# Attention over rows of 128 tokens: one maximum and one shift for the first group, merged copies of g and of P x, three exponentials ahead of a copy

## The chip, the core and the metric

The kernel runs on one NeuronCore of a Trainium2 chip. The metric is the device time of one execution in microseconds (us). Before the change it is 4721.29 us, the median of three runs (4721.06 to 4724.11). All tensors are 32-bit floats.

The engines that matter: TensorE (PE in the profile; PEld are its weight loads), VectorE (DVE), ScalarE (ACT), GpSimd (POOL), and the queue of SyncE (SP) that issues the DMAs. Each runs its own list of instructions in order, and they wait for one another by semaphores.

## The reference, cut to what matters

```python
xn = (x - moving_mean) * rsqrt(moving_var + 0.001) * gamma + beta   # x: (64, 128, 128, 64)
q = xn @ Wq + bq;  k = xn @ Wk + bk;  v = xn @ Wv + bv
scores = einsum('bhid,bhjd->bhij', q, k) * 64 ** -0.5               # 128 x 128 for each (b, h)
attn = softmax(scores, axis=-1)
out = einsum('bhij,bhjd->bhid', attn, v) @ Wo + bo
return xn + out
```

There are 64*128 = 8192 independent attentions, each over 128 tokens of 64 channels.

## The kernel before

The weights are folded once at the start: with g = (Wq Wk^T)^T x + a bias, the scores of one attention are one product of g and x, and the output is (P x) times one folded matrix, with P the softmax. So the loop never forms q, k or v.

Work comes in groups of 8 attentions (N = 1024 groups), and every engine's list is made of the same steps, one for two groups: the even group 2t and the odd group 2t+1. 512 steps do the work, and each engine's step handles several groups at different stages. `pipeline` (L177) writes out the first 12 steps and the last 8, and loops over bodies of 4 steps between.

What each engine does in a step, in its order:

- TensorE: transposes P of the even group before (`transpose_probs`, into `tg_ps`); scores of the even group (into `score_ps[0]`) and of the odd group (into `score_ps[1]`), the last pair of the odd ones behind a wait; transposes P of the odd group before; P x of two older groups (`probs_times_x`, into `uo_ps[0]` and `uo_ps[1]`, which also gives `u_made`); the two projections g of the next groups (`project`, into the two halves of `tg_ps`); the two output products (`output`, back into `uo_ps`), of which the last pair stands behind a wait for the copies of g, since the transposes that follow overwrite `tg_ps`.
- ScalarE: half of a copy of the transposed P (L349); two exponentials of the even group (L335; an exponential handles one attention, and its bias is `neg_top`, the negated shift of each row); a whole copy of the odd P (L351); the other six exponentials of the even group; two copies of g (`keep_g`, L360); eight exponentials of the odd group. A group's scores may be overwritten only when its eight exponentials are over (`probs_found`).
- VectorE: scaling of an older output by the inverted sums; its half of the copy of the transposed P (L549); inverted sums; then for the even group the maximum of attentions 0 to 3 (L490), their shift (L501), the maximum of attentions 4 to 7 (L490), their shift (L501); the maximum of the odd group in one (L480); the two copies of P x to SBUF (`keep_u`, L521); the shift of the odd group (L511); a transposition of incoming x for two groups (L559); a row constant (L530); and a scaling. In every second step (`vector_adds`) this last scaling is in place (L455) and is followed by the addition of x (L466), which GpSimd does otherwise.
- GpSimd weighs x, adds the bias, and adds x to three outputs in four. SyncE's queue loads x twice in two layouts and stores the results.

`tg_ps` is used in turn by the projections and by both transposes; `uo_ps[0]` and `uo_ps[1]` by P x and by the output product of the same group. `uT` has one place for an even group and one for an odd.

Of the kernel before, what the change touches and what calls it, by code (L numbers as in the profile page):

```python
# [17 lines left out]
def build(nc: bass.Bass, x, gamma, beta, mean, var, wq, bq, wk, bk, wv, bv, wo, bo, out):  # L18
# [12 lines left out]
    with ExitStack() as ctx:  # L31
# [3 lines left out]
        def psum(name, shape=(128, 512)):  # L35
            return ctx.enter_context(nc.psum_tensor(name, list(shape), F32))
# [57 lines left out]
        tg_ps = psum("tg_ps", (128, 2, 512))  # L94
        uo_ps = [psum(f"uo_ps{i}") for i in range(2)]
        score_ps = [psum(f"score_ps{i}", (128, 2, 512)) for i in range(2)]
# [12 lines left out]
        max_found = sem_ring("max_found")  # L109
        max_a_found = sem_ring("max_a_found")  # L110
        max_b_found = sem_ring("max_b_found")
        neg_const_found = sem_ring("neg_const_found")
        neg_top_found = sem_ring("neg_top_found")
        neg_top_a_found = sem_ring("neg_top_a_found")
        neg_top_b_found = sem_ring("neg_top_b_found")
        const_found = sem_ring("const_found")
# [196 lines left out]
        def _(act):  # L313
# [9 lines left out]
            def exponentials(r, n, peeled, rows):  # L323
                if not exists(r, n, peeled):
                    return
                s = parts(n)
                if 0 in rows:
                    act.wait_ge((neg_top_a_found if n % 2 == 0 else neg_top_found)[s], uses(r, n))
                    if exists(r, n - 4, peeled):
                        act.wait_ge(probsT_made[s], uses(r, n - 4))  # L330
                        act.wait_ge(sum_inverted[parts(n | 1)], uses(r, (n - 4) | 1))
                for q in rows:
                    if q == HALF and n % 2 == 0:
                        act.wait_ge(neg_top_b_found[s], uses(r, n))
                    last = nc.scalar.activation(probs[:, n % 4, q, :], score_ps[n % 2][:, q // PAIRS, q % PAIRS * W:(q % PAIRS + 1) * W],  # L335
                                                ACT.Exp, bias=neg_top[:, s, q:q + 1], accum_out=prob_sum[:, s, q:q + 1])
                    if q == GROUP - 1:
                        last.then_inc(probs_found[s], 1)
# [13 lines left out]

            def keep_g(r, n, peeled):
                if not exists(r, n, peeled):
                    return
                s = parts(n)
                act.wait_ge(g_made[s], uses(r, n))
                if exists(r, n - 4, peeled):
                    act.wait_ge(scores_made[s], uses(r, n - 4))
                nc.scalar.activation(g[:, s].rearrange("p k w -> p (k w)"), tg_ps[:, n % 2],  # L360
                                     ACT.Identity, bias=g_bias[:, 0:1]).then_inc(g_kept[s], 1)

            def step(r, t, peeled):
                keep_probsT(r, 2 * t - 2, peeled)
                exponentials(r, 2 * t, peeled, range(0, 2))
                keep_probsT(r, 2 * t - 1, peeled)
                exponentials(r, 2 * t, peeled, range(2, 8))
                keep_g(r, 2 * t + 2, peeled)
                keep_g(r, 2 * t + 3, peeled)
                exponentials(r, 2 * t + 1, peeled, range(0, 8))  # L370

# [3 lines left out]
        def _(dve):  # L375
# [107 lines left out]

            def find_max_half(r, n, peeled, h):
                if not exists(r, n, peeled):
                    return
                s = parts(n)
                if h == 0:
                    dve.wait_ge(scores_made[s], uses(r, n))
                nc.vector.tensor_reduce(row_stat[:, s, h * HALF:(h + 1) * HALF, NEG_MAX],  # L490
                                        score_ps[n % 2][:, h, :].rearrange("p (k w) -> p k w", k=PAIRS),
                                        AX_X, ALU.max, negate=True).then_inc((max_a_found if h == 0 else max_b_found)[s], 1)

            def find_shift_half(r, n, peeled, h):
                if not exists(r, n, peeled):
                    return
                s = parts(n)
                dve.wait_ge((max_a_found if h == 0 else max_b_found)[s], uses(r, n))
                if h == 0:
                    dve.wait_ge(neg_const_found[parts(n | 1)], uses(r, n | 1))  # L500
                nc.vector.tensor_reduce(neg_top[:, s, h * HALF:(h + 1) * HALF],  # L501
                                        row_stat[:, s, h * HALF:(h + 1) * HALF, NEG_MAX:ROW_CONST + 1], AX_X,
                                        ALU.add).then_inc((neg_top_a_found if h == 0 else neg_top_b_found)[s], 1)

            def find_shift(r, n, peeled):
# [7 lines left out]

            def keep_u(r, n, peeled):
                if not exists(r, n, peeled):
                    return
                s = parts(n)
                dve.wait_ge(u_made[s], uses(r, n))
                if exists(r, n - 2, peeled):
                    dve.wait_ge(o_made[parts(n - 2)], uses(r, n - 2))  # L520
                nc.vector.tensor_copy(uT[:, n % 2], uo_ps[n % 2][:].rearrange("p (k w) -> p k w", k=PAIRS)) \  # L521
                    .then_inc(u_kept[s], 1)
# [39 lines left out]
            def step(r, t, peeled):  # L562
# [3 lines left out]
                negate_const(r, 2 * t + 1, peeled)  # L566
                for h in range(2):
                    find_max_half(r, 2 * t, peeled, h)
                    find_shift_half(r, 2 * t, peeled, h)
                find_max(r, 2 * t + 1, peeled)  # L570
                keep_u(r, 2 * t - 4, peeled)
                keep_u(r, 2 * t - 3, peeled)
# [12 lines left out]
        def _(pe):  # L585
# [27 lines left out]
            def scores(r, n, peeled, pairs):  # L613
# [3 lines left out]
                if 0 in pairs:  # L617
                    pe.wait_ge(g_kept[s], uses(r, n))
                    if exists(r, n - 2, peeled):
                        pe.wait_ge(probs_found[parts(n - 2)], uses(r, n - 2))  # L620
# [26 lines left out]
            def await_transposes(r, n, peeled):  # L647
# [7 lines left out]
                if n % 2 == 0:  # L655
                    if exists(r, n + 3, peeled):
                        pe.wait_ge(g_kept[parts(n + 2)], uses(r, n + 2))
                        pe.wait_ge(g_kept[parts(n + 3)], uses(r, n + 3))
                else:
                    pe.wait_ge(probsT_b_kept[parts(n - 1)], uses(r, n - 1))  # L660
# [12 lines left out]
            def project(r, n, peeled):  # L673
# [6 lines left out]
                elif exists(r, n - 2, peeled):  # L680
                    pe.wait_ge(g_kept[parts(n - 2)], uses(r, n - 2))
                nc.tensor.matmul(tg_ps[:, n % 2], w_g_all, xT[:, n % 8].rearrange("p k w -> p (k w)"),  # L682
                                 start=True, stop=True).then_inc(g_made[s], 1)

            def output(r, n, peeled, pairs):
# [3 lines left out]
                if 0 in pairs:  # L689
                    pe.wait_ge(u_kept[s], uses(r, n))  # L690
                for k in pairs:
# [41 lines left out]
```

## Time and profile before

| | us |
|---|---|
| median of 3 runs | 4721.29 |
| the profiled execution's own time | 4727.12 |
| its span in the trace | 4724.9 |
| busy: PE | 4540.1 |
| busy: DVE | 4495.3 |
| busy: POOL | 4508.7 |
| busy: ACT | 4297.6 |

The span is what the trace covers; the execution's own time has some 2 us more around it. Four engines are busy for over 90% of the span, so the table alone names no bound. TensorE was granted its full clock (mean 0.998). A busy figure counts instructions from start to end, and on VectorE and ScalarE the end of one overlaps the start of the next, so the distance from start to start is what an instruction occupies.

### The profile page before, as it was taken

What the parts mean: (1) busy time and instruction counts of PE and PEld (TensorE: products, weight loads), DVE (VectorE), ACT (ScalarE), POOL (GpSimd) and SP (SyncE); (2) the same over time, 40 slices, a digit from 0 to 9 for tenths busy, and PEclk for the clock granted to TensorE, in tenths of its full rate; (3) what the DMA queues carried; (4) which work ended last, traced back from release to release, by engine and by line L of the source; (5) the groups of instructions that cost most, each with busy time, mean ns of one, the idle gap of its engine ahead of it and who ended that gap; (6) DMA issues with size and microseconds to landing.
All of it is one profiled execution on the core that took longest, in us unless ns stands there. A gap on an engine that the chain in (4) does not pass through costs nothing.

```text
span 4724.9 us, 187136 instructions
## 1 busy us (share of the span) xinstructions
PE 4540.1 (96%) x59416; PEld 3778.9 (80%) x59416; DVE 4495.3 (95%) x7970; ACT 4297.6 (91%) x18437; POOL 4508.7 (95%) x2824
## 2 busy tenths in 40 slices
PE   7999999999999999999999999999999999999999
PEld 5888888888888888888888888888888888888887
DVE  7999999999999999999999999999999999999998
ACT  7999999999999999999999999999999999999998
POOL 7999999999999999999999999999999999999998
PEclk9999999999999999999999999999999999999999
DMA  7888888888888888888888888888888888888886
GB/s 141 174 173 172 173 172 172 172 173 172 173 171 172 172 172 172 172 173 173 171 173 173 172 173 171 172 172 172 172 172 172 173 171 172 173 172 173 171 173 139
DMA packets 4294236, 806.28 MB, mean 171 GB/s; under 512 B 4294208, under 2 KB 4294208, under 8 KB 4294208
## 3 DMA queue, kind: packets, MB, share of 16 engines
q1 hardware_dynamic: 4293312, 805.80, 85.3%
q8 instruction: 15, 0.25, 0.0%
q10 hardware_dynamic: 896, 0.13, 0.0%
q14 instruction: 13, 0.11, 0.0%
HBM read 537.10 MB, written 268.44 MB: 170 GB/s over the span
## 4 chain that ended last, share of the span: by engine, by line
ACT 36%; DVE 26%; PE 20%; issue 15%; DVEq 2%; POOL 1%; DMA 0%; ACTq 0%; POOLq 0%
ACT probs L335 29%; PE uo_ps L643 10%; DVE xT L559 7%; PE score_ps L624 6%; ACT probsT L351 5%; DVE row_stat L530 5%; DVE uo_ps L455 4%; DVE probsT L549 3%; DVE row_stat L490 3%; ACT g L360 3%; PE tg_ps L670 3%; DVE attn L446 2%; DVE neg_top L501 1%; DVE inv_sum L473 1%; PE tg_ps L682 1%
## 5 line engine op out<-in xcount | busy, mean ns | idle before, releaser
L335 ACT ACTIVATE probs<-score_ps,neg_top 128x128 f32<-128x128 f32 x8192 | 2890.5, 384 | 301.9 <-DVE neg_top L501 301.9
L277 POOL TENSOR_TENSOR x_weighted<-x_in,row_weights 128x1024 f32<-128x1024 f32 x1024 | 2402.7, 2371 | 21.8 <-DVE x_weighted L433 21.8
L335 ACT ACTIVATION_READ_ACCUMULATOR probs<-score_ps,neg_top 128x1 f32 x8192 | 1835.5, 224 | 0.0
L624 PE MATMUL score_ps<-xT,g 64*128 64x128 f32 x16384 | 1165.3, 281 | 152.3 <-ACT probs L335 152.3
L624 PEld LDWEIGHTS score_ps<-xT,g 64*128 64x128 f32 x16384 | 1015.1, 188 | 236.9 <-issue 235.4
L288 POOL TENSOR_TENSOR x_scaled_rows<-x_weighted,out_bias 128x512 f32<-128x512 f32 x1024 | 1199.9, 1199 | 0.0
L692 PEld LDWEIGHTS uo_ps<-w_o,uT 128*128 128x128 f32 x8192 | 994.9, 192 | 244.0 <-issue 243.7
L299 POOL TENSOR_TENSOR y<-attn,x_scaled_rows 128x512 f32<-128x512 f32 x768 | 982.3, 1279 | 190.8 <-DVE attn L446 190.8
L682 PE MATMUL tg_ps<-xT,w_g 128*128 128x512 f32 x2048 | 1019.2, 620 | 4.7 <-DVE xT L559 3.5
L643 PE MATMUL uo_ps<-probsT,x_in 128*64 128x128 f32 x16384 | 1008.5, 276 | 0.0
L692 PE MATMUL uo_ps<-w_o,uT 128*128 128x128 f32 x8192 | 997.4, 275 | 0.0
L643 PEld LDWEIGHTS uo_ps<-probsT,x_in 128*64 128x64 f32 x16384 | 884.9, 137 | 34.7 <-issue 0.2
L521 DVE COPY uT<-uo_ps 128x512 f32<-128x512 f32 x1024 | 687.8, 687 | 91.4 <-PE uo_ps L643 74.3
L360 ACT ACTIVATE g<-tg_ps,g_bias 128x512 f32<-128x512 f32 x1024 | 706.6, 711 | 45.8 <-PE tg_ps L682 16.9
L670 PE MATMUL tg_ps<-ident,probs 64*128 64x64 f32 x16384 | 719.3, 226 | 5.3 <-ACT g L360 3.2
L490 DVE TENSOR_REDUCE row_stat<-score_ps 128x4 f32<-128x512 f32 x1024 | 699.3, 683 | 17.5 <-PE score_ps L624 0.9
L670 PEld LDWEIGHTS tg_ps<-ident,probs 64*128 64x128 f32 x16384 | 634.4, 139 | 69.2 <-issue 5.6
L559 DVE STREAM_TRANSPOSE xT<-x_quads 128x1024 f32<-128x1024 f32 x512 | 631.5, 1234 | 0.0
L480 DVE TENSOR_REDUCE row_stat<-score_ps 128x8 f32<-128x1024 f32 x512 | 622.6, 1216 | 1.7 <-PE score_ps L624 1.7
L682 PEld LDWEIGHTS tg_ps<-xT,w_g 128*128 128x128 f32 x2048 | 347.8, 189 | 338.3 <-issue 337.7
L530 DVE TENSOR_REDUCE row_stat<-x_weighted 128x16 f32<-128x1040 f32 x512 | 611.2, 1194 | 2.1 <-POOL x_weighted L277 2.1
L351 ACT ACTIVATE probsT<-tg_ps 128x1024 f32<-128x1024 f32 x512 | 524.1, 1024 | 57.3 <-PE tg_ps L670 57.3
(70 smaller groups left out, 2019.1 us busy)
## 6 DMA issues: line engine op xcount, KB each, us to landing
x_quads<-in_x SPq DMA_DIRECT2D x4096, 64.0 KB, 2.2
x_in<-in_x SPq DMA_DIRECT2D x1024, 256.0 KB, 3.2
out<-y SPq DMA_DIRECT2D x1024, 256.0 KB, 2.4
norm_row<-in_L_conv_gamma ACTq DMA_DIRECT2D x1, 32.0 KB, 2.1
norm_row<-in_L_conv_beta ACTq DMA_DIRECT2D x1, 32.0 KB, 3.7
norm_row<-in_L_conv_bo SPq DMA_DIRECT2D x1, 32.0 KB, 3.4
norm_row<-in_L_conv_moving_mean ACTq DMA_DIRECT2D x1, 32.0 KB, 3.3
norm_row<-in_L_conv_moving_var ACTq DMA_DIRECT2D x1, 32.0 KB, 4.6
```

The source lines that it names most:

```text
L277: nc.gpsimd.tensor_tensor(x_weighted[:, n % 4, :, 0:2 * C].rearrange("p s (h c) -> p s h c", h=2), x_in[:, n % 8, :, None, :].broadcast_to ...
L288: nc.gpsimd.tensor_tensor(x_scaled_rows[:, n % 8], x_weighted[:, n % 4, :, 0:C], bias_b, ALU.add).then_inc(x_scaled[s], 1)
L299: nc.gpsimd.tensor_tensor(y[:, s], attn[:, s], x_scaled_rows[:, n % 8], ALU.add).then_inc(y_found[s], 1)
L335: last = nc.scalar.activation(probs[:, n % 4, q, :], score_ps[n % 2][:, q // PAIRS, q % PAIRS * W:(q % PAIRS + 1) * W], ACT.Exp, bias=neg_ ...
L360: nc.scalar.activation(g[:, s].rearrange("p k w -> p (k w)"), tg_ps[:, n % 2], ACT.Identity, bias=g_bias[:, 0:1]).then_inc(g_kept[s], 1)
L530: nc.vector.tensor_reduce(row_stat[:, s - 1:s + 1, :, ROW_CONST], x_weighted[:, s - 1:s + 1, :, C:2 * C + 1], AX_X, ALU.add).then_inc(cons ...
L559: nc.vector.transpose(xT[:, n % 8 - 1:n % 8 + 1].rearrange("p g k w -> p (g k w)"), x_quads[:, n % 8 - 1:n % 8 + 1].rearrange("p g k w -> ...
L624: last = nc.tensor.matmul(score_ps[n % 2][:, h, k * W:(k + 1) * W], g[half, s, k, :], xT[half, n % 8, k, :], start=True, stop=True)
L643: last = nc.tensor.matmul(uo_ps[n % 2][h * C:(h + 1) * C, k * W:(k + 1) * W], x_in[:, n % 8, PAIRS * h + k, :], probsT[:, n % 4, PAIRS * h ...
L670: last = nc.tensor.transpose(tg_ps[:, h, q * C:(q + 1) * C], probs[half, n % 4, q, :], ident[half, half])
L682: nc.tensor.matmul(tg_ps[:, n % 2], w_g_all, xT[:, n % 8].rearrange("p k w -> p (k w)"), start=True, stop=True).then_inc(g_made[s], 1)
L692: last = nc.tensor.matmul(o_pairs[n % 2][:, :, k, :], uT[:, n % 2, k, :], w_o_all, start=True, stop=True)
```

## The change

Four edits, all inside a step:

- VectorE finds the even group's maximum for all eight attentions in one operation of 1024 elements, and its shift in one (`find_max`, `find_shift`), as it does for the odd group. The half versions and their semaphores go. ScalarE's first exponential of the even group waits for that one shift.
- The two copies of P x are one of 128x1024 (`uo_ps` is now one tensor of two banks), which waits for both products. TensorE's two output products wait for that one copy.
- The two copies of g are one of 128x1024, which waits for both projections. It stands behind the first two exponentials of the odd group, where the two copies stood ahead of them.
- Three exponentials of the even group, in place of two, stand ahead of the whole copy of the odd P.

```diff
             def step(r, t, peeled):
                 keep_probsT(r, 2 * t - 2, peeled)
-                exponentials(r, 2 * t, peeled, range(0, 2))
+                exponentials(r, 2 * t, peeled, range(0, 3))
                 keep_probsT(r, 2 * t - 1, peeled)
-                exponentials(r, 2 * t, peeled, range(2, 8))
-                keep_g(r, 2 * t + 2, peeled)
+                exponentials(r, 2 * t, peeled, range(3, 8))
+                exponentials(r, 2 * t + 1, peeled, range(0, 2))
                 keep_g(r, 2 * t + 3, peeled)
-                exponentials(r, 2 * t + 1, peeled, range(0, 8))
+                exponentials(r, 2 * t + 1, peeled, range(2, 8))
...
+                act.wait_ge(g_made[parts(n - 1)], uses(r, n - 1))
                 act.wait_ge(g_made[s], uses(r, n))
...
-                nc.scalar.activation(g[:, s].rearrange("p k w -> p (k w)"), tg_ps[:, n % 2],
+                nc.scalar.activation(g[:, s - 1:s + 1].rearrange("p n k w -> p (n k w)"), tg_ps[:].rearrange("p n x -> p (n x)"),
                                      ACT.Identity, bias=g_bias[:, 0:1]).then_inc(g_kept[s], 1)
...
+                dve.wait_ge(u_made[parts(n - 1)], uses(r, n - 1))
                 dve.wait_ge(u_made[s], uses(r, n))
                 if exists(r, n - 2, peeled):
+                    dve.wait_ge(o_made[parts(n - 3)], uses(r, n - 3))
                     dve.wait_ge(o_made[parts(n - 2)], uses(r, n - 2))
-                nc.vector.tensor_copy(uT[:, n % 2], uo_ps[n % 2][:].rearrange("p (k w) -> p k w", k=PAIRS)) \
+                nc.vector.tensor_copy(uT[:].rearrange("p n k w -> p (n k w)"), uo_both[:].rearrange("p n x -> p (n x)")) \
                     .then_inc(u_kept[s], 1)
...
-                for h in range(2):
-                    find_max_half(r, 2 * t, peeled, h)
-                    find_shift_half(r, 2 * t, peeled, h)
+                find_max(r, 2 * t, peeled)
+                find_shift(r, 2 * t, peeled)
                 find_max(r, 2 * t + 1, peeled)
-                keep_u(r, 2 * t - 4, peeled)
                 keep_u(r, 2 * t - 3, peeled)
...
-                    pe.wait_ge(g_kept[s], uses(r, n))
+                    pe.wait_ge(g_kept[parts(n | 1)], uses(r, n | 1))
...
-                        pe.wait_ge(g_kept[parts(n + 2)], uses(r, n + 2))
                         pe.wait_ge(g_kept[parts(n + 3)], uses(r, n + 3))
...
-                    pe.wait_ge(u_kept[s], uses(r, n))
+                    pe.wait_ge(u_kept[parts(n | 1)], uses(r, n | 1))
```

VectorE in a step with the addition in place, before the change, from the copy of the transposed P to the end of the step (`score_ps0` holds the even group, `score_ps1` the odd; the digit at a semaphore is its place in a ring):

```order
L549 COPY probsT<-tg_ps 128x8x64 [waits u_made0,probsT_made0]
L473 RECIPROCAL inv_sum<-prob_sum 128x16 [waits probs_found3]
L538 TENSOR_REDUCE row_stat<-row_stat 128x16 [waits const_found3]
L490 TENSOR_REDUCE row_stat<-score_ps0 128x4 [waits scores_made2]
L501 TENSOR_REDUCE neg_top<-row_stat 128x4 [waits neg_const_found3,max_a_found2]
L490 TENSOR_REDUCE row_stat<-score_ps0 128x4
L501 TENSOR_REDUCE neg_top<-row_stat 128x4 [waits max_b_found2]
L480 TENSOR_REDUCE row_stat<-score_ps1 128x8 [waits scores_made3]
L521 COPY uT<-uo_ps0 128x512 [waits o_made0,u_made2]
L521 COPY uT<-uo_ps1 128x512 [waits o_made1,u_made3]
L511 TENSOR_REDUCE neg_top<-row_stat 128x8 [waits neg_const_found3,max_found3]
L559 STREAM_TRANSPOSE xT<-x_quads 128x1024 [waits scores_made1,quads_loaded5,quads_loaded4]
```

The same place of VectorE's list after the change:

```order
L529 COPY probsT<-tg_ps 128x8x64 [waits u_made0,probsT_made0]
L471 RECIPROCAL inv_sum<-prob_sum 128x16 [waits probs_found3]
L518 TENSOR_REDUCE row_stat<-row_stat 128x16 [waits const_found3]
L478 TENSOR_REDUCE row_stat<-score_ps0 128x8 [waits scores_made2]
L488 TENSOR_REDUCE neg_top<-row_stat 128x8 [waits neg_const_found3,max_found2]
L478 TENSOR_REDUCE row_stat<-score_ps1 128x8 [waits scores_made3]
L501 COPY uT<-uo_ps 128x1024 [waits o_made0,o_made1,u_made3,u_made2]
L488 TENSOR_REDUCE neg_top<-row_stat 128x8 [waits neg_const_found3,max_found3]
L539 STREAM_TRANSPOSE xT<-x_quads 128x1024 [waits scores_made1,quads_loaded5,quads_loaded4]
```

Four operations on the even group have become two, and the first value of its shift now stands behind a reduction of 1024 elements. The two copies of P x, each with its own `u_made`, have become one that waits for both.

ScalarE over one step before the change, from the first exponential of an even group to the exponentials of the odd one:

```order
L335 ACTIVATE probs,prob_sum<-score_ps0,neg_top 128x128 [waits sum_inverted3,probsT_made2,neg_top_a_found2]
L335 ACTIVATE probs,prob_sum<-score_ps0,neg_top 128x128
L351 ACTIVATE probsT<-tg_ps 128x1024 [waits u_made1,probsT_made1]
L335 ACTIVATE probs,prob_sum<-score_ps0,neg_top 128x128 x2
L335 ACTIVATE probs,prob_sum<-score_ps0,neg_top 128x128 [waits neg_top_b_found2]
L335 ACTIVATE probs,prob_sum<-score_ps0,neg_top 128x128 x3
L360 ACTIVATE g<-tg_ps,g_bias 128x512 [waits scores_made0,g_made0]
L360 ACTIVATE g<-tg_ps,g_bias 128x512 [waits scores_made1,g_made1]
L335 ACTIVATE probs,prob_sum<-score_ps1,neg_top 128x128 [waits sum_inverted3,probsT_made3,neg_top_found3]
L335 ACTIVATE probs,prob_sum<-score_ps1,neg_top 128x128 x7
```

The same stretch of ScalarE after the change:

```order
L330 ACTIVATE probs,prob_sum<-score_ps0,neg_top 128x128 [waits sum_inverted3,probsT_made2,neg_top_found2]
L330 ACTIVATE probs,prob_sum<-score_ps0,neg_top 128x128 x2
L346 ACTIVATE probsT<-tg_ps 128x1024 [waits u_made1,probsT_made1]
L330 ACTIVATE probs,prob_sum<-score_ps0,neg_top 128x128 x5
L330 ACTIVATE probs,prob_sum<-score_ps1,neg_top 128x128 [waits sum_inverted3,probsT_made3,neg_top_found3]
L330 ACTIVATE probs,prob_sum<-score_ps1,neg_top 128x128
L358 ACTIVATE g<-tg_ps,g_bias 128x1024 [waits scores_made0,scores_made1,g_made1,g_made0]
L330 ACTIVATE probs,prob_sum<-score_ps1,neg_top 128x128 x6
```

The copy of g has moved behind two exponentials of the odd group, and these wait for the odd group's shift, which VectorE computes behind the copy of P x.

## Rows read from the trace of the kernel before

**Rows 1.** The head of the profile page: span, and busy time of each engine.

```profile
span 4724.9 us, 187136 instructions
PE 4540.1 (96%) x59416; PEld 3778.9 (80%) x59416; DVE 4495.3 (95%) x7970; ACT 4297.6 (91%) x18437; POOL 4508.7 (95%) x2824
```

**Rows 2.** Chain of waits, from 1996 us on: start us, us on the chain, what.

```profile
1996.24 1.16 PE score_ps L624 x16
...
1999.85 0.04 DVE uT L521
...
2000.46 0.04 DVE neg_top L511
...
2005.79 0.60 DVE row_stat L490
...
2006.61 0.03 ACT probs L335
...
2014.53 1.16 PE score_ps L624 x16
```

**Rows 3.** The same chain near its beginning and near its end, the same piece.

```profile
205.10 1.16 PE score_ps L624 x16
...
4500.21 1.16 PE score_ps L624 x16
```

**Rows 4.** Waits: engine, line waited for: us in total, times, longest us.

```profile
ACT probs L335 <- DVE neg_top L501: 301.9, 510, 1.8
PE score_ps L624 <- ACT probs L335: 152.3, 511, 1.1
DVE uT L521 <- PE uo_ps L643: 74.3, 401, 3.7
```

**Rows 5.** Groups of instructions by line: busy us, mean ns of one, idle before.

```profile
L521 DVE COPY uT<-uo_ps 128x512 f32<-128x512 f32 x1024 | 687.8, 687 | 91.4 <-PE uo_ps L643 74.3
L360 ACT ACTIVATE g<-tg_ps,g_bias 128x512 f32<-128x512 f32 x1024 | 706.6, 711 | 45.8 <-PE tg_ps L682 16.9
...
L490 DVE TENSOR_REDUCE row_stat<-score_ps 128x4 f32<-128x512 f32 x1024 | 699.3, 683 | 17.5 <-PE score_ps L624 0.9
...
L480 DVE TENSOR_REDUCE row_stat<-score_ps 128x8 f32<-128x1024 f32 x512 | 622.6, 1216 | 1.7 <-PE score_ps L624 1.7
...
L351 ACT ACTIVATE probsT<-tg_ps 128x1024 f32<-128x1024 f32 x512 | 524.1, 1024 | 57.3 <-PE tg_ps L670 57.3
...
L349 ACT ACTIVATE probsT<-tg_ps 128x512 f32<-128x512 f32 x512 | 331.5, 648 | 0.0
```

**Rows 6.** Timeline of ScalarE at the copies of g: start us, us, instructions merged.

```profile
2010.27 1.32 ACT L360 ACTIVATE g<-tg_ps,g_bias 128x512 f32<-128x512 f32 x2
2011.47 0.38 ACT L335 ACTIVATE probs<-score_ps,neg_top 128x128 f32<-128x128 f32 x1
...
2011.81 0.38 ACT L335 ACTIVATE probs<-score_ps,neg_top 128x128 f32<-128x128 f32 x1
```

**Rows 7.** Timeline of TensorE and VectorE over the same step and the next start.

```profile
2005.38 1.16 PE L624 MATMUL score_ps<-xT,g 64*128 64x128 f32 x16 [0.29 <-ACT probs L335]
...
2005.70 0.67 DVE L490 TENSOR_REDUCE row_stat<-score_ps 128x4 f32<-128x512 f32 x1
...
2007.29 1.22 DVE L480 TENSOR_REDUCE row_stat<-score_ps 128x8 f32<-128x1024 f32 x1
...
2008.42 1.28 DVE L521 COPY uT<-uo_ps 128x512 f32<-128x512 f32 x2
...
2008.86 1.98 PE L682 MATMUL tg_ps<-xT,w_g 128*128 128x512 f32 x4
...
2009.62 0.17 DVE L511 TENSOR_REDUCE neg_top<-row_stat 128x8 f32<-128x24 f32 x1
...
2013.11 1.11 PE L624 MATMUL score_ps<-xT,g 64*128 64x128 f32 x16
...
2014.27 0.69 DVE L490 TENSOR_REDUCE row_stat<-score_ps 128x4 f32<-128x512 f32 x1
```

More of the change, by code:

```diff
@@ L94, in build @@
         tg_ps = psum("tg_ps", (128, 2, 512))
-        uo_ps = [psum(f"uo_ps{i}") for i in range(2)]
+        uo_both = psum("uo_ps", (128, 2, 512))
+        uo_ps = [uo_both[:, i] for i in range(2)]
         score_ps = [psum(f"score_ps{i}", (128, 2, 512)) for i in range(2)]
@@ L109, in build @@
         max_found = sem_ring("max_found")
-        max_a_found = sem_ring("max_a_found")
-        max_b_found = sem_ring("max_b_found")
         neg_const_found = sem_ring("neg_const_found")
         neg_top_found = sem_ring("neg_top_found")
-        neg_top_a_found = sem_ring("neg_top_a_found")
-        neg_top_b_found = sem_ring("neg_top_b_found")
         const_found = sem_ring("const_found")
@@ L327, in exponentials @@
                 if 0 in rows:
-                    act.wait_ge((neg_top_a_found if n % 2 == 0 else neg_top_found)[s], uses(r, n))
+                    act.wait_ge(neg_top_found[s], uses(r, n))
                     if exists(r, n - 4, peeled):
@@ L332, in exponentials @@
                 for q in rows:
-                    if q == HALF and n % 2 == 0:
-                        act.wait_ge(neg_top_b_found[s], uses(r, n))
                     last = nc.scalar.activation(probs[:, n % 4, q, :], score_ps[n % 2][:, q // PAIRS, q % PAIRS * W:(q % PAIRS + 1) * W],
@@ L356, in keep_g @@
                 s = parts(n)
+                act.wait_ge(g_made[parts(n - 1)], uses(r, n - 1))
                 act.wait_ge(g_made[s], uses(r, n))
                 if exists(r, n - 4, peeled):
+                    act.wait_ge(scores_made[parts(n - 5)], uses(r, n - 5))
                     act.wait_ge(scores_made[s], uses(r, n - 4))
-                nc.scalar.activation(g[:, s].rearrange("p k w -> p (k w)"), tg_ps[:, n % 2],
+                nc.scalar.activation(g[:, s - 1:s + 1].rearrange("p n k w -> p (n k w)"), tg_ps[:].rearrange("p n x -> p (n x)"),
                                      ACT.Identity, bias=g_bias[:, 0:1]).then_inc(g_kept[s], 1)
@@ L482, in find_max @@
                                         AX_X, ALU.max, negate=True).then_inc(max_found[s], 1)
[L484 to L503, printed above, removed]
             def find_shift(r, n, peeled):
@@ L680, in project @@
                 elif exists(r, n - 2, peeled):
-                    pe.wait_ge(g_kept[parts(n - 2)], uses(r, n - 2))
+                    pe.wait_ge(g_kept[parts((n - 2) | 1)], uses(r, (n - 2) | 1))
                 nc.tensor.matmul(tg_ps[:, n % 2], w_g_all, xT[:, n % 8].rearrange("p k w -> p (k w)"),
```

## The prediction, made before the changed kernel ran

> **What bounds the kernel now.** I read the page's head first: four engines between 91% and 96% busy [rows 1]. Shares so close name no bound, and an edit that saves busy time on one engine need not save anything. So the next view is the chain of waits, which shows what really follows what. It repeats every two steps, and its turn is this loop:
>
> - TensorE starts the scores of an odd group at 1996.24; P x of the older odd group is made behind them, and VectorE starts the second copy of P x at 1999.85, 3.61 us later.
> - The copy is over at 2000.46, where the odd shift starts (0.61 us). VectorE then works through its list (transposition, constant, scaling, addition, the next step's scaling and copy) to the first half maximum of the next even group: it starts at 2005.70 [rows 7] (the chain counts it from 2005.79). That is 5.24 us in which VectorE never stands still for another engine.
> - Half a maximum and its shift, and ScalarE starts the first exponential at 2006.61: 0.91 us.
> - ScalarE runs eight exponentials of the even group, a copy, two copies of g, eight of the odd group; when these are over, TensorE may overwrite the odd scores: 2014.53, 7.92 us later, where the loop closes [rows 2].
>
> Sum: 3.61 + 0.61 + 5.24 + 0.91 + 7.92 = 18.29 us for two steps. Over the whole run: from 205.10 to 4500.21 there are 235 such turns, so 18.28 us each [rows 3], and 256 turns are 4679 us of the 4724.9. So this loop is the kernel. It always passes through the same kind of step, the one whose VectorE list has the addition in place. In the other kind VectorE is just in time: the first maximum starts at 2014.27, when the scores started at 2013.11 (1.11 us) are ready [rows 7].
>
> The waits agree with it. ScalarE waits 301.9 us for the shift, 0.59 us a step, and TensorE 152.3 us for the exponentials, 0.30 us a step [rows 4]. Without waiting, TensorE needs from 2005.38 to 2014.22 (2013.11 + 1.11) for all but the last matmuls of a step, 8.84 us [rows 7]. It is close behind but not the bound.
>
> **The change part by part, each on this loop.**
>
> One maximum for the even group. The first exponential now waits for a reduction of 1024 elements, not 512: 1216 ns against 683 ns, by rows of these very shapes [rows 5]. The start comes 0.53 us later: **+0.53 us a turn**. ScalarE is the waiting engine there [rows 4], so nothing hides it. What VectorE gains, the distance from the first half's start to the odd maximum, was 1.59 us (2005.70 to 2007.29) [rows 7] and becomes some 1.22 + 0.17 = 1.39: 0.20 us saved. But that comes ahead of the copy of P x, where VectorE then waits for TensorE. On this loop it is worth nothing.
>
> One copy of P x. The second of two copies (687 ns) started when its product was made; now the whole copy starts then, and the first half, which was done while TensorE made the second product, follows the wait as well. No row shows a copy of 1024 elements on VectorE. The bounds: the 687 ns of the short one (nothing lost), and twice it, 1374 ns. The nearest row is the maximum over the same 1024 elements from the same memory, 1216 ns, whose short form (683) matches the short copy's 687 [rows 5]. I take 1.22 us: 1.22 - 0.69 = **+0.53 us a turn**. Its reward is 0.06 us of VectorE's time where two copies ran back to back (2008.42 to 2009.62 is 1.20 us [rows 7]; one would take about 1.22 less the 0.08 of overlap, 1.14), and again it lies ahead of no late work: behind the copy VectorE's 5.24 us are unchanged, so the next maximum is late by the whole amount. The output products wait for this copy too: it ends 3.61 + 1.26 = 4.87 us behind the start of the odd scores, and TensorE reaches them at 2008.86 + 1.98 - 2005.38 = 5.46. That wait costs nothing, with 0.6 us to spare.
>
> One copy of g. Two copies took from 2010.27 to 2011.47, 1.20 us, and their records end 0.12 us later [rows 6]. The long copy of P on ScalarE takes 1024 ns and the short 648; I add that difference to the 711 ns of a copy of g: 1.09 us, and 0.97 us to the next start [rows 5]. **-0.23 us a turn**. The bounds: 1.20 us (nothing gained) and 0.71 us, the short one's (-0.49).
>
> What a page says of the two merges: the Trainium skill (Perfetto Trace Analysis, Optimizing Scalar/DVE Operations) gives each such instruction a fixed access cost, some 125 ns on VectorE and 51 ns on ScalarE where it reads PSUM, and says that grouping helps "if the engine is saturated". The trace has both engines above 90% busy, and yet ScalarE waits at this point in every step [rows 4], so its condition isn't met where the time is set; by its sum the change would be a gain, which is the faster rival below.
>
> The order on ScalarE. Moving one exponential ahead of the copy of P changes nothing in the sum: the same instructions lie between the first exponential and the last; nothing here waits for the copy soon enough to matter (TensorE needs it only behind both P x products, and 0.35 us later). Moving g behind two exponentials of the odd group likewise keeps the sum, if these find their shift. The shift now comes from the long copy: 3.61 + 0.04 + 1.22 + 0.20 = 5.07 us behind the start of the odd scores. In the loop's step ScalarE reaches them about 6 us behind: the maximum starts there 3.61 + 1.14 + 5.24 = 9.99 us behind the odd scores of the step before, which is 0.9 us behind the next ones if these follow after 9.10; then come 1.44 us to the first exponential, eight exponentials at 0.34 [rows 6] and 0.9 for the copy of P (1.02 less 0.12 of overlap), 5.96 in all. No wait. g then needs both projections, made 5.46 us behind: also there. In the other kind of step the shift is the later one, and ScalarE waits; that loop is priced with the rivals.
>
> **The sum.** 18.28 + 0.53 + 0.53 - 0.23 = 19.11 us a turn, +0.83. With 254 turns (the first and the last two steps are not in the pattern): +211 us. Against the profiled execution, 4727.12 us, that is 4938; the median of the runs shown lies 5.8 us below it, so **4932 us**, 4.5% slower. Its own range comes from the bounds that matter: g between 0.88 and 1.05 to the next start (-23 to +20 us) and the long copy of P x at 1.10 to 1.28 us (-30 to +15): 4880 to 4970. With the far ends of both rows of bounds it would be 4730 (the copy costs nothing more and g gains 0.49) and 5030.
>
> **The rivals.**
>
> Faster: the engines' work carries the time, not this loop. Then VectorE saves 0.20 + 0.06 = 0.26 us a step, ScalarE 0.23, and 512 x 0.26 = 133 us come off: 4588. For it: the busy shares, all over 90% [rows 1], and the copies of P x that start back to back without a wait in one step of two [rows 7], which looks like a VectorE that is late for its work. It decides if the long copy can start on VectorE's own clock in both kinds of step. Against it: DVE waited for P x 401 times in 512 steps [rows 4], and the change makes VectorE arrive earlier and its input complete later. Chance 0.07.
>
> Only one of the two delays counts: the copy of P x gives its time back, say because VectorE's list behind it holds a pause that I can't see. Then 0.53 - 0.23 = 0.30 us a turn, +76: 4797. For it: the chain has pieces named as issue in that stretch. Against: the starts lie as close there as the instructions allow. Chance 0.06.
>
> A new loop is the bound: the odd exponentials ahead of g wait for the shift in every step: 3.61 + 1.26 + 0.20, two exponentials 0.69, g 0.97, and six exponentials with their end (2011.47 to 2014.53 less 0.69) 2.37: 9.10 us for one step, 18.20 for two. Less than 19.11, so it only shapes the other step. It would need 0.46 us more a step to decide; and TensorE's transposes, which wait for g, then follow at 6.9 us behind the maximum. If these close a loop with the late step that I haven't priced, the turn grows by up to the 0.5 us between them, +60 to +130 us: about 5025. Chance 0.03.
>
> No change: the two delays fall into pauses and g's gain is cancelled too: 4721, chance 0.03.
>
> **How the numbers follow.** Forecast 0.81, faster rival 0.07, one delay 0.06, new loop 0.03, no change 0.03. A measurement of this kernel can't tell less than about 0.2% (9 us) from no change. Faster by more: 0.07. Same: 0.03. Slower: 0.81 + 0.06 + 0.03 = 0.90. The range 4860 to 4980 holds the forecast's own with some room and leaves out the other cases, 0.19 together; to take in one more of them it would have to reach 4797.
>
> **What would show it.** ScalarE's wait for the shift grows from 302 us to about 600 to 700, part of it now ahead of the odd exponentials. VectorE's wait for P x grows from 74 us to some 300: in one kind of step it arrives 1.2 us early, in the other hardly. TensorE's wait for the exponentials goes to about 400. The chain shows the same loop with 19.1 us, with pieces of 1.2 us for the copy and the even maximum. Lines: even maximum 1.22 us, copy of P x 1.22, copy of g 1.09. The prediction is wrong if the turn isn't about 19.1 us or the chain leaves the copy of P x; its terms are wrong if the long copy takes much less than 1.2 us.

## The result, and the profile of the changed kernel

The changed kernel takes **4954.69 us** (median of three runs, 4954.67 to 4954.86), against 4721.29: a ratio of 1.0493, 95% interval 1.0469 to 1.0516. It is slower by 233 us. The forecast was 4932. One execution of one of the kernels below (`g_only`) ran at a granted clock of 0.851 and took 5265 us; it is left out of that kernel's figure.

The head of its page, beside [rows 1]:

```profile
span 4952.5 us, 184581 instructions
PE 4671.2 (94%) x59416; PEld 3843.6 (78%) x59416; DVE 4357.8 (88%) x6434; ACT 4147.0 (84%) x17925; POOL 4505.2 (91%) x2824
```

VectorE's busy time fell by 138 us and ScalarE's by 151 us, and the span rose by 228 us. The merges did save engine time; none of it shows.

Waits (engine, line waited for: us in total, times, longest), to be read beside [rows 4]; L330 is the exponential, L488 the shift, L501 the copy of P x, L621 P x, L346 the whole copy of the transposed P, L659 the projection:

```profile
ACT probs L330 <- DVE neg_top L488: 762.9, 512, 3.7
...
DVE uT L501 <- PE uo_ps L621: 280.1, 259, 2.7
PE tg_ps L659 <- ACT probsT L346: 189.8, 256, 1.6
...
DVE uT L501 <- issue: 120.3, 253, 0.6
...
PEld score_ps L602 <- issue: 79.6, 387, 0.6
```

ScalarE's wait for the shift went from 302 to 763 us. VectorE's idle time ahead of the copy of P x went from 91 us [rows 5] to 400 (both rows on L501; its copy waits for four semaphores, and in half of the steps the profile calls the wait issue). TensorE's wait of 152 us for the exponentials is no longer a row of its matmuls; what is left of it stands at the weight loads of the scores, where the profile calls it issue (L602, the last row; the part on the prediction comes back to it). A wait of 190 us for ScalarE's copy has come.

Groups (busy us, mean ns of one, idle before), beside [rows 5]:

```profile
L478 DVE TENSOR_REDUCE row_stat<-score_ps 128x8 f32<-128x1024 f32 x1024 | 1246.1, 1217 | 19.3 <-PE score_ps L602 3.0
...
L501 DVE COPY uT<-uo_ps 128x1024 f32<-128x1024 f32 x512 | 626.9, 1224 | 400.4 <-PE uo_ps L621 280.1
...
L358 ACT ACTIVATE g<-tg_ps,g_bias 128x1024 f32<-128x1024 f32 x512 | 600.8, 1173 | 16.7 <-PE tg_ps L659 16.6
```

The timeline of one turn of two steps, from the start of one odd group's scores to the one two steps on (start us, us, instructions merged), beside [rows 2, 6, 7]:

```profile
1994.42 1.00 PEld L602 LDWEIGHTS score_ps<-xT,g 64*128 64x128 f32 x16 [0.21 <-issue]
...
1998.10 1.22 DVE L501 COPY uT<-uo_ps 128x1024 f32<-128x1024 f32 x1 [1.08 <-PE uo_ps L621]
...
2004.41 1.21 DVE L478 TENSOR_REDUCE row_stat<-score_ps 128x8 f32<-128x1024 f32 x1
...
2005.86 0.37 ACT L330 ACTIVATE probs<-score_ps,neg_top 128x128 f32<-128x128 f32 x1 [1.84 <-DVE neg_top L488]
...
2008.08 1.96 PE L659 MATMUL tg_ps<-xT,w_g 128*128 128x512 f32 x4 [0.74 <-ACT probsT L346]
...
2010.20 1.17 ACT L358 ACTIVATE g<-tg_ps,g_bias 128x1024 f32<-128x1024 f32 x1
...
2011.20 0.43 ACT L330 ACTIVATE probs<-score_ps,neg_top 128x128 f32<-128x128 f32 x1
...
2013.16 0.31 ACT L330 ACTIVATION_READ_ACCUMULATOR probs<-score_ps,neg_top 128x1 f32 x1
...
2013.58 1.00 PEld L602 LDWEIGHTS score_ps<-xT,g 64*128 64x128 f32 x16 [0.20 <-issue]
...
2017.27 1.23 DVE L501 COPY uT<-uo_ps 128x1024 f32<-128x1024 f32 x1 [1.07 <-PE uo_ps L621]
```

From copy to copy, 1998.10 to 2017.27, a turn is 19.17 us; it was 18.28. 254 turns of 0.89 are 226 us, all but 2 us of the difference of the spans (227.6).

The chain of waits, however, doesn't go by the copy of P x in this stretch (start us, us on the chain, what):

```profile
1993.93 0.10 POOL x_weighted L274
1994.04 2.22 issue
1996.25 2.38 POOL x_weighted L274
1998.63 0.03 issue
1998.66 0.02 DVEq L509
1998.68 0.56 issue
1999.24 0.17 DVE neg_top L488
```

It names GpSimd. L509 is VectorE's wait ahead of the row constant (L510), which its queue handled while the long copy was running, and the shift at 1999.24 starts when that copy lets it: 1.14 us behind 1998.10. That VectorE waited for GpSimd is contradicted by a row of the groups, with 1.3 us of idle time in the whole run:

```profile
L510 DVE TENSOR_REDUCE row_stat<-x_weighted 128x16 f32<-128x1040 f32 x512 | 610.9, 1193 | 1.3 <-POOL x_weighted L274 1.3
```

Still, a chain that leaves the copy was what the prediction named as a sign against itself, so the loop had to be shown by experiment.

### The profile page after: what moved, and what is told of

The parts are those of the page before. It is cut to its first block, busy times and chain, and to the rows that moved or that the text cites. A ratio compares the mean times of both kernels' runs of the same rounds, so it can differ in the third digit from the quotient of the medians.

```text
span 4952.5 us, 184581 instructions
## 1 busy us (share of the span) xinstructions
PE 4671.2 (94%) x59416; PEld 3843.6 (78%) x59416; DVE 4357.8 (88%) x6434; ACT 4147.0 (84%) x17925; POOL 4505.2 (91%) x2824
## 4 chain that ended last, share of the span: by engine, by line
DVE 41%; issue 29%; POOL 14%; ACT 9%; PE 4%; DVEq 1%; POOLq 1%; DMA 0%; ACTq 0%
POOL x_weighted L274 13%; DVE xT L539 12%; DVE row_stat L510 8%; DVE row_stat L478 6%; DVE attn L444 6%; ACT probs L330 5%; ACT probsT L346 5%; DVE uo_ps L453 4%; PE tg_ps L659 3%; DVE probsT L529 3%; DVE neg_top L488 2%; DVE inv_sum L471 1%; POOL y L296 1%; DVE y L464 0%; POOLq L295 0%
## 5 line engine op out<-in xcount | busy, mean ns | idle before, releaser
L330 ACT ACTIVATE probs<-score_ps,neg_top 128x128 f32<-128x128 f32 x8192 | 2926.8, 413 | 763.0 <-DVE neg_top L488 762.9
L330 ACT ACTIVATION_READ_ACCUMULATOR probs<-score_ps,neg_top 128x1 f32 x8192 | 2072.6, 253 | 0.0
L478 DVE TENSOR_REDUCE row_stat<-score_ps 128x8 f32<-128x1024 f32 x1024 | 1246.1, 1217 | 19.3 <-PE score_ps L602 3.0
L669 PEld LDWEIGHTS uo_ps<-w_o,uT 128*128 128x128 f32 x8192 | 1032.8, 191 | 294.4 <-issue 182.4
L659 PE MATMUL tg_ps<-xT,w_g 128*128 128x512 f32 x2048 | 1002.7, 612 | 229.4 <-ACT probsT L346 189.8
L602 PE MATMUL score_ps<-xT,g 64*128 64x128 f32 x16384 | 1189.6, 284 | 18.0 <-ACT g L358 1.3
L602 PEld LDWEIGHTS score_ps<-xT,g 64*128 64x128 f32 x16384 | 1044.2, 188 | 97.9 <-issue 79.6
L669 PE MATMUL uo_ps<-w_o,uT 128*128 128x128 f32 x8192 | 1081.6, 279 | 4.2 <-DVE uT L501 4.1
L621 PE MATMUL uo_ps<-probsT,x_in 128*64 128x128 f32 x16384 | 1007.5, 276 | 0.0
L501 DVE COPY uT<-uo_ps 128x1024 f32<-128x1024 f32 x512 | 626.9, 1224 | 400.4 <-PE uo_ps L621 280.1
L621 PEld LDWEIGHTS uo_ps<-probsT,x_in 128*64 128x64 f32 x16384 | 883.9, 137 | 34.7 <-issue 0.2
L659 PEld LDWEIGHTS tg_ps<-xT,w_g 128*128 128x128 f32 x2048 | 347.5, 189 | 583.3 <-issue 583.3
L358 ACT ACTIVATE g<-tg_ps,g_bias 128x1024 f32<-128x1024 f32 x512 | 600.8, 1173 | 16.7 <-PE tg_ps L659 16.6
L444 DVE TENSOR_TENSOR attn<-uo_ps,inv_sum 128x512 f32<-128x512 f32 x768 | 528.2, 688 | 95.9 <-PE uo_ps L669 94.0
L510 DVE TENSOR_REDUCE row_stat<-x_weighted 128x16 f32<-128x1040 f32 x512 | 610.9, 1193 | 1.3 <-POOL x_weighted L274 1.3
L346 ACT ACTIVATE probsT<-tg_ps 128x1024 f32<-128x1024 f32 x512 | 526.0, 1027 | 1.2 <-PE tg_ps L647 1.2
```

The lines of the kernel that those rows point to most:

```text
L478: nc.vector.tensor_reduce(row_stat[:, s, :, NEG_MAX].rearrange("p (h k) -> p h k", h=2), score_ps[n % 2][:].rearrange("p h (k w) -> p h k ...
L510: nc.vector.tensor_reduce(row_stat[:, s - 1:s + 1, :, ROW_CONST], x_weighted[:, s - 1:s + 1, :, C:2 * C + 1], AX_X, ALU.add).then_inc(cons ...
L602: last = nc.tensor.matmul(score_ps[n % 2][:, h, k * W:(k + 1) * W], g[half, s, k, :], xT[half, n % 8, k, :], start=True, stop=True)
L621: last = nc.tensor.matmul(uo_ps[n % 2][h * C:(h + 1) * C, k * W:(k + 1) * W], x_in[:, n % 8, PAIRS * h + k, :], probsT[:, n % 4, PAIRS * h ...
L669: last = nc.tensor.matmul(o_pairs[n % 2][:, :, k, :], uT[:, n % 2, k, :], w_o_all, start=True, stop=True)
```

## The experiments

Each is given with the difference to the kernel before as measured beside it (4724.9, 4723.0 or 4726.1 us); for the changed kernel the difference is +233. "A turn" is the difference over 254.

**One edit at a time.** Four kernels, each the kernel before with one part of the change.

The maximum and shift of the even group in one (`max_only`):

```diff
-                for h in range(2):
-                    find_max_half(r, 2 * t, peeled, h)
-                    find_shift_half(r, 2 * t, peeled, h)
+                find_max(r, 2 * t, peeled)
+                find_shift(r, 2 * t, peeled)
```

> The kernel before with one edit: one maximum and one shift for the even group. Loop theory (the time is one loop of two steps, through the copy of P x, VectorE's list behind it, the even maximum and ScalarE): the first exponential comes 0.53 us later in each of 254 turns, +135 us, 4856 us. Work theory (the time is what the busy engines have to do): VectorE saves 0.20 us in each of 512 steps, so 4619 us, or no change if another engine bounds.

Measured: 4844.84 us, ratio 1.0253 (1.0236 to 1.0270); +120, 0.47 us a turn. VectorE's own saving bought nothing. The work theory, which allowed a gain or no change, falls.

The one copy of P x (`u_only`), as in the change:

```diff
-                keep_u(r, 2 * t - 4, peeled)
                 keep_u(r, 2 * t - 3, peeled)
```

> The kernel before with one edit: one copy of P x of 128x1024, which waits for both products. Loop theory: the copy starts when the second of two did and takes 0.53 us longer, +135 us, 4856 us. Work theory: VectorE saves 0.06 us a step, 4690 us.

Measured: 4867.13 us, ratio 1.0301 (1.0284 to 1.0318); +142, 0.56 us a turn. Its timeline has the turn between two copies of the same kind of step, 18.79 us, and in each the copy's wait for the second product:

```profile
1999.85 1.23 DVE L524 COPY uT<-uo_ps 128x1024 f32<-128x1024 f32 x1 [1.18 <-PE uo_ps L645]
...
2018.64 1.23 DVE L524 COPY uT<-uo_ps 128x1024 f32<-128x1024 f32 x1 [1.18 <-PE uo_ps L645]
```

The one copy of g at its old place (`g_only`):

```diff
-                keep_g(r, 2 * t + 2, peeled)
                 keep_g(r, 2 * t + 3, peeled)
                 exponentials(r, 2 * t + 1, peeled, range(0, 8))
```

> The kernel before with one edit: one copy of g of 128x1024, at the place of the two. Loop theory: in the changed kernel this copy takes 1.00 us to the next start, 0.20 less than the two, on the loop: -51 us, 4670 us. Rival: the single copy waits for both projections at this place and gives the gain back, 4721 us or more.

Measured: 4965.62 us, ratio 1.0510 (1.0489 to 1.0531); +241. The loop theory's number was far off, and its rival's mechanism is what the timeline shows:

```profile
2008.64 1.16 PE L625 MATMUL score_ps<-xT,g 64*128 64x128 f32 x16 [0.73 <-ACT probs L335]
...
2014.20 1.11 ACT L362 ACTIVATE g<-tg_ps,g_bias 128x1024 f32<-128x1024 f32 x1 [0.74 <-issue]
...
2018.25 1.16 PE L625 MATMUL score_ps<-xT,g 64*128 64x128 f32 x16 [0.73 <-ACT probs L335]
```

ScalarE stands 0.74 us before the copy, until the second projection is done. That closes a loop of one step: odd scores, P x, projections (5.56 us), the copy and eight exponentials (4.05): 9.61 us, twice 9.61 for two steps. So one merge alone, at the wrong place, costs as much as the whole change.

ScalarE's order alone (`order_only`):

```diff
-                exponentials(r, 2 * t, peeled, range(0, 2))
+                exponentials(r, 2 * t, peeled, range(0, 3))
...
-                exponentials(r, 2 * t, peeled, range(2, 8))
+                exponentials(r, 2 * t, peeled, range(3, 8))
+                exponentials(r, 2 * t + 1, peeled, range(0, 2))
                 keep_g(r, 2 * t + 2, peeled)
                 keep_g(r, 2 * t + 3, peeled)
-                exponentials(r, 2 * t + 1, peeled, range(0, 8))
+                exponentials(r, 2 * t + 1, peeled, range(2, 8))
```

> The kernel before with only ScalarE's order changed: three exponentials ahead of the whole copy of P, and two exponentials of the odd group ahead of the two copies of g; nothing merged. Loop theory: the same instructions lie on the loop and none waits longer, 4721 us within 10. Rival: the moved waits for the odd shift or the later copy of P hold ScalarE or TensorE and this is part of the loss, 4760 us or more.

Measured: 4714.83 us, ratio 0.9978 (0.9968 to 0.9987); -10. As good as nothing, with a small gain.

**The one copy of g with its new place** (`g_moved`): the edits of `g_only` and `order_only` together.

> The kernel before with one copy of g standing behind two exponentials of the odd group, and three exponentials ahead of the copy of P; maxima and copies of P x as before. Loop theory: alone at its old place the one copy of g waited for the second projection in every step and closed a loop of one step (9.61 us); behind two exponentials that wait is gone and the 0.20 us a turn are left as a gain: 4665 to 4680 us. Rival: the wait for both projections or the odd shift still holds ScalarE, 4725 us or more.

Measured: 4673.40 us, ratio 0.9897 (0.9880 to 0.9914); -50, the 0.20 us a turn. The move behind two exponentials is what makes the merge of g pay. The parts' sum, 120 + 142 - 50 = 212 us, leaves 21 of the 233 to the parts' being together, and why is open.

**One part undone** (`no_max`): the changed kernel with the halves back.

```diff
-                find_max(r, 2 * t, peeled)
-                find_shift(r, 2 * t, peeled)
+                for h in range(2):
+                    find_max_half(r, 2 * t, peeled, h)
+                    find_shift_half(r, 2 * t, peeled, h)
```

> The changed kernel with the even group's maximum and shift in halves again, all else as changed. Loop theory: the edits add up on one loop, so it gives back what the one maximum alone cost (120 us measured, 0.47 a turn): 4835 us, between 4820 and 4840. Rival: the edits act on different loops, and with the long copy of P x in place the halves bring little, 4900 us or more.

Measured: 4829.74 us, ratio 1.0218 (1.0201 to 1.0235); +104. The halves give back 130 us, as one maximum alone had cost 120. The delays add up to within 10 us, as on one loop.

**A known cost put into the loop, and beside it.** If the time is a loop through VectorE's list in only one kind of step, one and the same operation must cost its whole length there and nothing in the other. First an operation with both inputs from SBUF (`spend_a` in the steps with the addition in place, `spend_b` in the others):

```diff
                 transpose_x(r, 2 * t + 7, peeled)
+                if vector_adds(2 * t - 4):      # spend_b: if not vector_adds(2 * t - 4)
+                    spend(r, 2 * t - 4, peeled)
...
+                    nc.vector.tensor_tensor(spare[:], ident[:, None, :].broadcast_to([128, 4, 128]),
+                                            ident[:, None, :].broadcast_to([128, 4, 128]), ALU.mult)
```

> The changed kernel with one more VectorE operation of 128x512 (0.69 us, 0.60 to the next start) behind the transposition of x, in the steps with the addition in place. Loop theory: all of it is on the loop, 254 x 0.60 = +152 us over the changed kernel. Work theory: VectorE is busy for 88% only, so little or nothing, or the same as in the other kind of step.

> The changed kernel with the same additional VectorE operation in the other steps, as often and as long. Loop theory: VectorE stands there 0.37 us ahead of a scaling, and the rest is not on the loop: 0 to +60 us. Work theory: the same as with the operation in the steps with the addition.

Measured: `spend_a` 5209.14 us, ratio 1.1031 (1.1012 to 1.1049); `spend_b` 5174.70 us, ratio 1.0956 (1.0938 to 1.0974). Both are far above what was expected, and the first reading is that the loop theory has failed. The timelines give the reason. In `spend_a`:

```profile
2001.12 1.05 DVE L507 TENSOR_TENSOR spare<-ident 128x512 f32<-128x512 f32 x1
2002.10 1.22 DVE L516 TENSOR_REDUCE row_stat<-x_weighted 128x16 f32<-128x1040 f32 x1
```

and in `spend_b`, with GpSimd beside it:

```profile
2017.27 2.32 POOL L286 TENSOR_TENSOR x_scaled_rows<-x_weighted,out_bias 128x512 f32<-128x512 f32 x2
...
2018.40 1.74 DVE L507 TENSOR_TENSOR spare<-ident 128x512 f32<-128x512 f32 x1
2020.07 1.22 DVE L516 TENSOR_REDUCE row_stat<-x_weighted 128x16 f32<-128x1040 f32 x1
```

The operation wasn't the one I meant: it took 0.98 us of VectorE in the one and 1.67 in the other. By those sizes, `spend_a` pays 486 - 233 = 253 us for 254 x 0.98 = 249, all of it; `spend_b` pays 452 - 233 = 219, 0.86 a turn of the 1.67 added, so 0.81 us were free there. That fits the loop, but a theory repaired after the fact needs a test of its own: a reduction, with one input, that should take 0.60 us of VectorE in both places.

```diff
-                    nc.vector.tensor_tensor(...)
+                    nc.vector.tensor_reduce(spare[:], ident[:, None, :].broadcast_to([128, 4, 128]), AX_X, ALU.max)
```

> The changed kernel with one more VectorE reduction of 128x512 from SBUF (some 0.68 us, 0.60 to the next start, no second input) behind the transposition of x, in the steps with the addition in place. Loop theory: all of it is on the loop, 254 x 0.60 = +152 us over the changed kernel, some 5107 us. Work theory: the same as in the other steps.

> The changed kernel with the same reduction in the other steps. Loop theory, with the slack that the longer operation left there (1.67 added, 0.87 paid, so 0.80 us free): nothing, 4955 us within 15. Work theory: the same +152 us.

Measured: `reduce_a` 5106.68 us, ratio 1.0805 (1.0787 to 1.0823), +381, so 147 us over the change. `reduce_b` 4957.43 us, ratio 1.0490 (1.0472 to 1.0507), +231: nothing, for the same work. The group's row in `reduce_a` (mean 645 ns; in `reduce_b` the median was 644) shows that this time the two were alike:

```profile
L507 DVE TENSOR_REDUCE spare<-ident 128x4 f32<-128x512 f32 x256 | 165.2, 645 | 0.0
```

A cost is paid in full in the steps with the addition (147 us of 152) and not at all in the others, which no account by busy time can tell apart. It also answers the chain that named GpSimd: the reduction stands ahead of the row constant, the operation whose wait for GpSimd the chain names. Had VectorE waited for GpSimd there, that wait would have covered the reduction.

**Taking work out of the loop.** The addition of x (0.69 us) moved out of VectorE's stretch ahead of the even maximum, to behind its shift; in the changed kernel (`after_late_add`), and with the one copy of g and all else as before, where it goes behind the first half's shift (`late_add_g`):

```diff
                 find_max(r, 2 * t, peeled)
                 find_shift(r, 2 * t, peeled)
+                if vector_adds(2 * t - 6):
+                    add_in_place(r, 2 * t - 6, peeled)
...
                     scale_in_place(r, 2 * t - 4, peeled)
-                    add_in_place(r, 2 * t - 4, peeled)
```

> The changed kernel with VectorE's addition of x moved from ahead of the next even maximum to behind its shift. Loop theory: 0.68 us leave the loop, and the other kind of step, with 0.80 us free, allows it: -173 us, 4782 us. Rival: the work is the same and TensorE's P x waits for the late addition, 4900 us or more.

Measured: 4917.50 us, ratio 1.0405 (1.0387 to 1.0422); +191. The gain over the change is 42 us, not 173. The rival's mechanism is what the timeline shows:

```profile
2010.20 0.69 DVE L464 TENSOR_TENSOR y<-uo_ps,x_scaled_rows 128x512 f32<-128x512 f32 x1
...
2010.95 1.97 PE L622 MATMUL uo_ps<-probsT,x_in 128*64 128x128 f32 x32 [0.59 <-DVE y L464]
```

The next P x overwrites what the addition reads. With the whole maximum ahead of it the addition ends at 2010.89, and TensorE waits 0.59 us for it in each turn (154 us in all); the turn is still 19.0 us. That a second loop, through this wait of TensorE, takes over is read from the wait and not tested by itself.

> A try at a faster kernel: the kernel before with one copy of g behind two exponentials, and with VectorE's addition of x moved from ahead of the next even maximum to behind the first half's shift, so that 0.69 us leave the loop. Loop theory: this loop falls to about 17.4 us and TensorE's 8.8 us a step or the other kind of step take over: 4570 to 4640 us. Rival: the work is the same, so no gain over the one copy of g; or TensorE's P x waits for the late addition, 4680 us or more.

Measured: 4644.46 us, ratio 0.9835 (0.9819 to 0.9852); -78, the fastest of all here, though 4 us outside the loop theory's range. With the halves the addition starts 0.9 us behind the maximum's start, and TensorE's wait for it is small (25 us in all, at its weight loads). The gain beyond the one copy of g is 29 us, less than the 0.68 us a turn that left the loop. The page's shares of the chain by line say where the time went next:

```profile
PE uo_ps L646 21%; PE tg_ps L684 21%; PE score_ps L627 20%; PE uo_ps L694 20%; PE tg_ps L672 11%; DVE row_stat L492 2%; DVE y L468 2%; POOL x_weighted L277 0%; POOL y L299 0%; ACT probs L335 0%; DVEq L467 0%; DVE neg_top L503 0%; DMA bias_col<-in_L_conv_bv 0%; POOL x_scaled_rows L288 0%; ACT g L362 0%
```

Five groups of TensorE make up 93% of it, so TensorE's own list is close to the bound. It is not free of waits, though: ahead of the scores its weight loads still stand idle for 79 us in all, as in the changed kernel. No further run tests what bounds this one.

## Why the prediction was right

Its sign and size held, and so did the loop: +211 forecast, +233 measured. Two of the signs that it named did not come: the chain leaves the copy of P x, and TensorE's wait for the exponentials fell where it was to rise. Step by step:

- **The bound** was one loop of two steps, not the busy shares. Shown by `reduce_a` and `reduce_b`; the sums of the parts agree.
- **One maximum, +0.53 us a turn.** 0.47 alone, 0.51 when undone in the changed kernel. The forecast was a little high.
- **One copy of P x, +0.53.** 0.56 alone. The length assumed from the reduction, 1.22 us, was measured at 1224 ns.
- **One copy of g, -0.23.** From start to next start it takes 1.00 us (2010.20 to 2011.20), not 0.97, so -0.20; `g_moved` agrees. Its record was 1173 ns, not 1090. The Trainium skill (ScalarE: Activation LUTs, What ACT_TABLE_LOAD costs) gives 280 + 0.833 N ns for an instruction with such a bias, an estimate of 1133 ns here; the runs lie on both sides, 1.11 us in `g_only` and 1.17 in the changed kernel.
- **The rest of the turn.** Measured: odd scores to copy 3.68, copy to maximum 6.31, to the exponential 1.45, to the next odd scores 7.72: 19.16. Forecast: 3.61, 6.38, 1.44, 7.69. The forecast was 0.05 us a turn short, 13 us of the 23 missed. Another 6 are the distance between profiled execution and median, which was 5.8 us before and nothing after. The small remainder is not explained. Seen by parts, the forecast's 211 us are the 212 that the parts cost alone; it had no term for the 21 us that they cost together.
- **The order on ScalarE.** The sum was right, but its reason was not: "nothing here waits for the copy soon enough to matter". TensorE's projections do wait for it, 0.74 us at 2008.08, in the very steps where the even exponentials start late. It is off the loop all the same: TensorE, late by this much, still comes to the odd scores too early.
- **TensorE's wait for the exponentials.** About 400 us forecast. It is smaller than before and has not gone. In the changed kernel the last odd exponential is over at 2013.47 (2013.16 + 0.31), and the weight load that it holds back starts at 2013.58, 0.11 us later, after 0.20 us of idle time. Before the change the same distance was 0.11 us too:

```profile
2014.12 0.26 ACT L335 ACTIVATION_READ_ACCUMULATOR probs<-score_ps,neg_top 128x1 f32 x1
...
2014.49 1.00 PEld L624 LDWEIGHTS score_ps<-xT,g 64*128 64x128 f32 x16 [0.47 <-issue]
```

So the loop closes where the prediction had it close. The forecast failed because TensorE now loses most of the time at its projections; their wait of 190 us has no place in the prediction.

- **Other waits.** ScalarE's for the shift: 600 to 700 forecast, 763 measured. VectorE's for P x: from 74 to some 300 forecast; 280 measured in the row of the same kind, 400 with the pauses called issue.
- **The rivals.** The faster one fell with `max_only` and `u_only`. What costs is merging at a place where another engine waits. The Trainium skill (Perfetto Trace Analysis, Optimizing Scalar/DVE Operations) also has this side, that where the engines aren't saturated but cause bubbles on others, breaking instructions up "may allow work to be completed sooner". `no_max` is such a case, with 130 us; VectorE was busy for 88% of the changed kernel. The new loop of one step, forecast at 9.10 us and not the bound, is real: without the two exponentials ahead of g, it is 9.61 us and the bound (`g_only`).

## What to carry to other kernels

Two halves in a row are a pipeline: the consumer starts after the first, and the first is done while the producer makes the second. Merging them saves a fixed cost on the engine, here 0.2 to 0.3 us a step, and puts the other half onto whoever waits, here 0.5 us a turn each time. Find the loop that sets the step, by adding the starts along it, and merge only off it; when a merged operation needs a later input, move it behind work that is ready, as the copy of g was. The cheapest proof of such a loop is one known operation put into it and then beside it.

## What the runs showed of the hardware

An operation of VectorE with 128x512 elements and both inputs in SBUF had a median record of 1050 ns in `spend_a` and of 1758 in `spend_b`; its shortest were 680 and 650 ns. Both times GpSimd was at work on two additions. In `spend_b` the operation started at 2018.40, when the first of them was about to end (2017.27 + 1.18), and ended at 2020.14, 0.55 us behind the end of the second (2019.59). In `spend_a` it started at 2001.12, in the middle of the first, and ended at 2002.17, 0.55 us behind that one's end (2000.44 + 1.18); the two additions then took 2.78 us in place of 2.32. A reduction with one SBUF input at the same two places took 645 ns in both. The Trainium skill (SBUF — State Buffer, SBUF: two separate sides) describes the pair of ports that VectorE's second input and GpSimd share as an exclusive lock, held for a whole instruction. Both times fit that: in each the operation ends as if it had waited for one addition, the second in `spend_b` and the first in `spend_a`, where the second addition then waited in its turn. It was met by accident and not isolated.
